# Two spills held back behind a weight load, four projection tiles issued in a row, and a split first pass over the output weights

## The reference

```python
x = x + attn(layernorm(x))      # a long convolution along the last axis (4096) with a kernel K
                                # computed from a 64-state model, plus D * u
x = x + ffn(layernorm(x))

def ffn(x):                     # K=64 experts of rank 16, top 16 of 64
    scores = x @ Wr.T
    top_vals, top_idx = top_k(scores, 16)
    G = scatter(softmax(top_vals))            # (rows, 64)
    h = einsum('nd,krd->nkr', x, A)           # (rows, 64, 16) = rows x 1024
    return 2.0 * einsum('nkr,kdr->nd', h * G[:, :, None], B)
```

## Time and profile before

| | |
|---|---|
| median of 3 runs | 1453.24 us (1449.32 to 1455.43) |
| profiled execution, own time | 1455.56 us |
| its span, slowest core (core 4) | 1453.9 us |
| the other cores' spans | 1441.7 to 1453.0 us |
| PE busy | 990.3 us (68%) |
| VectorE, ACT, POOL busy | 454.8, 193.8, 178.9 us |
| DMA | 186.60 MB, mean 128 GB/s |
| chain that ended last, by engine | PE 49%, DMA 13%, VectorE 11%, issue 9%, POOL 6% |

### The profile page before, as it was taken

One profiled execution on the slowest core, in us unless ns is written; L12 is line 12 of the kernel. 1 busy time (PEld: TensorE's weight loads), 2 busy tenths in 40 slices (PEclk: granted clock), 3 DMA queues, 4 the chain that ended last, 5 costly groups with the idle time before them and its releaser, 6 DMA issues.

```text
span 1453.9 us, 13339 instructions; the slowest of 8 cores (1441.7 to 1453.9 us)
## 1 busy us (share of the span) xinstructions
PE 990.3 (68%) x3837; PEld 395.3 (27%) x3837; DVE 454.8 (31%) x954; ACT 193.8 (13%) x402; POOL 178.9 (12%) x221
## 2 busy tenths in 40 slices
PE   1655347667676678355288768767876944999997
PEld 0133132112112222111133323322332411444443
DVE  2022126237337349302422132222212001334442
ACT  1300013342332433000100010010001000000000
POOL 6700000440440534000000000000000000000000
PEclk9855557879878889767688778977878976999999
DMA  6300006846638319998100030020006057679876
GB/s 119 137 0 0 7 1 231 290 145 214 231 134 269 101 37 225 214 168 215 74 1 0 0 116 1 0 84 33 0 1 108 9 138 214 224 282 302 287 268 251
DMA packets 28977, 186.60 MB, mean 128 GB/s; under 512 B 7976, under 2 KB 8745, under 8 KB 12906
## 3 DMA queue, kind: packets, MB, share of 16 engines
q1 hardware_dynamic: 9274, 84.52, 16.9%
q0 software_dynamic: 12720, 34.11, 13.7%
q10 hardware_dynamic: 6912, 67.11, 12.3%
HBM read 119.15 MB, written 83.89 MB: 140 GB/s over the span
## 4 chain that ended last, share of the span: by engine, by line
PE 49%; DMA 13%; DVE 11%; issue 9%; POOL 6%; another core or an unknown queue 5%; ACT 4%; DVEq 1%; ACTq 0%; POOLq 0%; SPq 0%
PE psA L978 16%; PE psA L1066 15%; DMA xsp_b<-U 7%; POOL sqs L272 4%; DMA Bt_hi<-bt_in 3%; PE ps L823 3%; DVE sqs L817 2%; PE psX L870 2%; DMA U<-u_in 2%; DVE cvt L727 2%; PE psA L711 1%; PE psS L688 1%; PE ps L277 1%; POOL wrt_b L369 1%
## 5 line engine op out<-in xcount | busy, mean ns | idle before, releaser
L978 PE MATMUL psA<-X,At_sb 128*128 128x512 bf16 x1024 | 252.8, 410 | 0.0
L1066 PE MATMUL psA<-htl_b,Bt_hi 128*128 128x512 bf16 x512 | 133.6, 383 | 42.2 <-DMA Bt_hi<-bt_in 42.2
L1073 DVE SCALAR_TENSOR_TENSOR XF<-psA,XF 128x512 f32<-128x512 f32 x128 | 88.5, 691 | 177.5 <-PE psA L1066 121.2
L978 PEld LDWEIGHTS psA<-X,At_sb 128*128 128x128 bf16 x1024 | 105.7, 105 | 138.9 <-issue 38.9
L272 POOL TENSOR_TENSOR sqs<-ubf 128x512 bf16<-128x512 bf16 x128 | 131.0, 1056 | 45.5 <-PE ps L277 31.4
L1066 PE MATMUL psA<-htl_a,Bt_lo 128*128 128x512 bf16 x512 | 132.5, 381 | 0.0
L264 PE MATMUL ps<-ubf,sumw 128*128 128x512 bf16 x128 | 61.0, 477 | 70.9 <-ACT ubf L259 70.8
L732 DVE TENSOR_TENSOR U<-U,cvt 128x512 f32<-128x512 f32 x128 | 89.9, 702 | 13.7 <-DVE cvt L727 0.5
L711 PE MATMUL psA<-ln1w,cm_T 128*128 128x512 bf16 x320 | 93.5, 391 | 0.0
L259 ACT CAST ubf<-U 128x512 bf16<-128x512 f32 x128 | 72.9, 615 | 154.8 <-PE ps L264 50.5
L727 DVE TENSOR_TENSOR cvt<-psA,Rb 128x512 f32<-128x512 f32 x128 | 87.6, 684 | 7.6 <-PE psA L717 7.6
(11 more groups left out here) (228 smaller groups left out, 694.6 us busy)
## 6 DMA issues: line engine op xcount, KB each, us to landing
U<-u_in SPq DMA_DIRECT2D x16, 2048.0 KB, 8.6
xsp_f<-U ACTq DMA_DIRECT2D x16, 2048.0 KB, 12.3
XF<-xsp_f SPq DMA_DIRECT2D x32, 1024.0 KB, 7.6
y_out<-XF ACTq DMA_DIRECT2D x32, 1024.0 KB, 7.4
xsp_b<-U POOLq DMA_DIRECT2D x16, 1024.0 KB, 12.9
X<-xsp_b SPq DMA_DIRECT2D x3, 4096.0 KB, 13.8
At_sb<-at_in POOLq DMA_DIRECT2D x32, 256.0 KB, 54.5
X<-xsp_b SPq DMA_DIRECT2D x2, 2048.0 KB, 11.7
```

The source lines that it names most:

```text
L978: P.op("tensor", lambda e, kr=kr, db=db, pb=pb, xb=xb: e.matmul(psA.ap()[:, pb * 512:(pb + 1) * 512], At_sb.ap()[:, db * 1024 + kr * 128:d ...
L1066: P.op("tensor", lambda e, d=d, kbo=kbo, kb=kb, pb=pb, s1=s1, bt=bt: e.matmul(psA.ap()[:, pb * 512:(pb + 1) * 512], bt.ap()[:, kbo * DM + ...
L1073: P.op("vector", lambda e, dd=dd, pb=pb, xf=xf: e.scalar_tensor_tensor(xf.ap()[:, dd * 512:(dd + 1) * 512], psA.ap()[:, pb * 512:(pb + 1) ...
```

## The change

Three edits.

1. In slice 3 of the convolution stage the spills of quarters 2 and 3, on ACT's and on POOL's queue, wait until all 16 transfers of `at2` have landed. SP's wait ahead of the load of slice 2 into X2[0] asks for 224 in place of 256 (slices 1 and 3 keep 256).
2. In slice 0 of the gated stage tiles 0 to 3 are issued as a block: their projection matmuls one after the other into the four banks of `psA` (with a wait for the gating before bank 3), then for each of the four the gate matmul into `psS`, ACT's copy and VectorE's product, then all eight preparation steps of slice 1. Tiles 4 to 7 go on as before, with two more waits for the products that free the banks.
3. In the first pass of the output stage tiles 0 to 3 use the four banks of `psA`: first the matmuls on `Bt_lo` for all four, then those on `Bt_hi`.

```diff
@@ convolution stage, after every second chunk @@
                 P.wait("scalar", "v_xe", vxe_b + 8 * (q + 1))
+                if s == 3 and q >= 2:
+                    P.wait("scalar", "at2", 16 * 16)
                 P.dma("scalar", lambda e, s=s, buf=buf, q=q: e.dma_start(
...
                 P.wait("gpsimd", "v_xe", vxe_b + 8 * (q + 1))
+                if s == 3 and q >= 2:
+                    P.wait("gpsimd", "at2", 16 * 16)
                 P.dma("gpsimd", lambda e, s=s, buf=buf, q=q: e.dma_start(
...
-        P.wait("sync", "spf", 256)
-        P.wait("sync", "spb", 256)
+        need2 = 224 if s % 2 == 0 else 256
+        P.wait("sync", "spf", need2)
+        P.wait("sync", "spb", need2)
@@ gated stage @@
-        for kr in range(8):
+        kr_start = 0
+        if s == 0:
+            kr_start = 4
+            for kr in range(4):
+                if kr == 3:
+                    P.wait("tensor", "gq", gq_done[0])
+                for db in range(NBLK):
+                    P.op("tensor", lambda e, kr=kr, db=db, xb=xb: e.matmul(
+                        psA.ap()[:, kr * 512:(kr + 1) * 512],
+                        At_sb.ap()[:, db * 1024 + kr * 128:db * 1024 + (kr + 1) * 128],
+                        blk_ap(xb, db), start=(db == 0), stop=False))
+                P.op("tensor", ...rank-1 correction..., inc="t_h")
+            for kr in range(4):
+                if kr >= 1:
+                    P.wait("tensor", "s_gp", kr)
+                P.op("tensor", ...gate matmul into psS..., inc="t_gr")
+                P.wait("scalar", "t_gr")
+                if kr >= 2:
+                    P.wait("scalar", "v_ht", kr - 1)
+                P.op("scalar", ...copy psS to grep..., inc="s_gp")
+                P.wait("vector", "t_h")
+                P.wait("vector", "s_gp")
+                P.op("vector", ...product into htl..., inc="v_ht")
+            for _ in range(8):
+                if nxt_steps:
+                    nxt_steps.pop(0)()
+
+        for kr in range(kr_start, 8):
...
+            if s == 0 and kr == 4:
+                P.wait("tensor", "v_ht", 3)
             P.wait("tensor", "gq", gq_done[s])
...
                 elif kr == 5:
+                    if s == 0:
+                        P.wait("tensor", "v_ht", 4)
                     sx_r2 = emit_chain2(s + 1, nb2)
@@ output stage @@
-        for dd in range(16):
+        if s2 == 0:
+            for dd in range(4):
+                if dd < 2:
+                    P.wait("tensor", "v_ht", htl_after[-1] - 1 + dd)
+                if dd == 0:
+                    P.wait("tensor", "btl", 16 * 4)
+                for kb in range(4):
+                    P.op("tensor", ...matmul on Bt_lo into bank dd, start=(kb == 0), stop=False...)
+            for dd in range(4):
+                for kb in range(4, 8):
+                    if dd == 0:
+                        P.wait("tensor", "bhi", 16 * (kb - 3))
+                    P.op("tensor", ...matmul on Bt_hi into bank dd, stop=(kb == 7)...,
+                        inc=("t_o" if kb == 7 else None))
+                P.wait("vector", "t_o")
+                P.wait("vector", "xfl", 16)
+                P.op("vector", ...residual add of bank dd..., inc="v_y")
+        for dd in range(4 if s2 == 0 else 0, 16):
```

More of the change, by code:

```diff
@@ L971, in build_nc @@
             nxt_steps, nb2 = emit_prep2(s + 1)
-        for kr in range(8):
+        kr_start = 0
[9 more added lines that the diff above has]
+                        blk_ap(xb, db), start=(db == 0), stop=False))
+                P.op("tensor", lambda e, kr=kr: e.matmul(
+                    psA.ap()[:, kr * 512:(kr + 1) * 512],
+                    A1row.ap()[0:1, kr * 128:(kr + 1) * 128],
+                    nm2.ap()[0:1, 0:512],
+                    start=False, stop=True), inc="t_h")
+            for kr in range(4):
+                if kr >= 1:
+                    P.wait("tensor", "s_gp", kr)
+                P.op("tensor", lambda e, kr=kr: e.matmul(
+                    psS.ap()[:, :], rghx.ap()[64:128, kr * 128:(kr + 1) * 128],
+                    ghx.ap()[64:128, 0:512], start=True, stop=True), inc="t_gr")
+                P.wait("scalar", "t_gr")
+                if kr >= 2:
+                    P.wait("scalar", "v_ht", kr - 1)
+                P.op("scalar", lambda e, kr=kr: e.copy(
+                    grep.ap()[:, (kr % 2) * 512:(kr % 2 + 1) * 512],
+                    psS.ap()[:, :]), inc="s_gp")
+                P.wait("vector", "t_h")
+                P.wait("vector", "s_gp")
+                P.op("vector", lambda e, kr=kr: e.tensor_mul(
+                    htl_ap(kr, 0, 512),
+                    psA.ap()[:, kr * 512:(kr + 1) * 512],
+                    grep.ap()[:, (kr % 2) * 512:(kr % 2 + 1) * 512]), inc="v_ht")
+            for _ in range(8):
+                if nxt_steps:
+                    nxt_steps.pop(0)()
+        for kr in range(kr_start, 8):
             pb = kr % 2
@@ L1050, in build_nc @@
         xf = XF[s2 % 2]
-        for dd in range(16):
+        if s2 == 0:
[5 more added lines that the diff above has]
+                for kb in range(4):
+                    P.op("tensor", lambda e, dd=dd, kb=kb: e.matmul(
+                        psA.ap()[:, dd * 512:(dd + 1) * 512],
+                        Bt_lo.ap()[:, kb * DM + dd * 128:kb * DM + (dd + 1) * 128],
+                        htl_ap(kb, 0, 512), start=(kb == 0), stop=False))
+            for dd in range(4):
+                for kb in range(4, 8):
+                    if dd == 0:
+                        P.wait("tensor", "bhi", 16 * (kb - 3))
+                    P.op("tensor", lambda e, dd=dd, kb=kb: e.matmul(
+                        psA.ap()[:, dd * 512:(dd + 1) * 512],
+                        Bt_hi.ap()[:, (kb - 4) * DM + dd * 128:(kb - 4) * DM + (dd + 1) * 128],
+                        htl_ap(kb, 0, 512), start=False, stop=(kb == 7)),
+                        inc=("t_o" if kb == 7 else None))
+                P.wait("vector", "t_o")
+                P.wait("vector", "xfl", 16)
+                P.op("vector", lambda e, dd=dd, xf=xf: e.scalar_tensor_tensor(
+                    xf.ap()[:, dd * 512:(dd + 1) * 512], psA.ap()[:, dd * 512:(dd + 1) * 512],
+                    2.0, xf.ap()[:, dd * 512:(dd + 1) * 512], ALU.mult, ALU.add), inc="v_y")
+        for dd in range(4 if s2 == 0 else 0, 16):
             d = 16 * g + dd
             pb = dd % 2
-            if s2 == 0 and dd < 2:
-                P.wait("tensor", "v_ht", htl_after[-1] - 1 + dd)
             if s2 * 16 + dd >= 2:
@@ L1060, in build_nc @@
                 kbo = kb % 4
[L1061 to L1065, removed]
                 P.op("tensor", lambda e, d=d, kbo=kbo, kb=kb, pb=pb, s1=s1, bt=bt: e.matmul(
```

## The result

The change is faster by 1.0%: a ratio of 0.9896 (95%: 0.9877 to 0.9914), which of 1453.6 us is 15.1 us (12.5 to 17.9). Ratios and intervals leave out slow executions, in which the cores of one half of the chip show a lower granted clock; of the ten after this was one, at 1532.4 us, and of the ten before none.

The account below looks back on a forecast made before the run. The load of X's second half bounds the gated stage's start, then PE with its helpers, then PE alone in the output. Gains 5 + 5.5 + 2.5 = 13.0 take 1455.56 to 1442.5 us (median 1440.2); range 1430 to 1450.

Parts of the forecast that it names:

- spills: Input of the gated stage: delayed spills let the load of X's second half land earlier; gain 5 us, bounds -4 and +10.
- tiles: Gated stage, slice 0: four tiles in a row, then gates and sums, 54.7 us for 60.2; gain 5.5, bounds 1.4 to 7.3.
- output: Output stage, first tiles: twelve matmuls run ahead of the last landing of B; gain 2.5 us, bounds 2.2 and 5.1.
- rival D: Gated stage, slice 0: low clock through all the sums; tiles gain 1.4 for 5.5, total 8.9, 1444.3 us; chance 0.12.
- E: Convolution's end: matrix A lands no faster, near 644, X's second half 11 us later; 1456 or 1463 us; chance 0.07.
- q 2 at once and q 3 when q 2 has landed: Tail of DMA behind matrix A: both delayed spills lie in it, adding 2 x 6.5 to 30.7 us, less 0 to 4.
- T: Convolution's end, slice 3: the time matrix A has landed, forecast about 628 us, 16 earlier; bounds 14 and 19 earlier.
- A: Whole kernel: the forecast itself holds, 1436 to 1444 us; chance 0.45.
- C: Tail of DMA: spills fill gaps, X's second half lands by 665; 10 or more, total 18, 1433 to 1436 us; chance 0.13.
- B: Tail of DMA: each spill costs 7 to 9 us; spills bring 0 to -4, total 4 to 8, 1445 to 1449; chance 0.2.
- I count five such pairs: Gated stage, slice 0: only five pairs of sum matmuls run at the low clock, 1.27 us apart against 1.03, adding 1.1.
- F: Gated stage, slice 0: four tiles run under the gating chain, PE's 15.67 us of waiting vanish; about 1425 us; chance 0.03.

Follow-up runs that it names:

- the early casts: The changed kernel with chunk 7's four casts issued on ACT ahead of its waiting spill: ratio 0.9899 to the kernel before, against the change's 0.9896.
- The two experiments on the clock: Changed kernel with each gate right behind its tile: ratio 0.9878 to the kernel before; changed kernel with slice 1's sums right behind tile 4's projection: 0.9859.

## Why the prediction was right, and where its sizes were off

The total was predicted at 13.0 and measured at 15.1. Each term in us against what it measured, on the slowest cores of the two profiled executions, as the mean of the cores, and by the edit alone:

| term | predicted | slowest cores | mean of the cores | edit alone |
|---|---|---|---|---|
| spills | 5 | 8.4 | 9.2 | 7.6 |
| tiles | 5.5 | 1.4 | 3.6 | 2.8 |
| output | 2.5 | 2.5 | 3.4 | 2.9 |
| sum | 13.0 | 12.3 | 16.2 | 13.3 |

The tiles' 1.4 is 60.2 - 58.1, less the 0.7 that tile 4 is longer (7.86 against 7.16). Its 3.6 is the time from the gating's last transpose to slice 1's scores, 69.5 before and 65.9 after. Two terms were off, in opposite directions, and the total is nearer than they are: that much of the agreement is luck. The clock did what rival D said, whose total was 8.9, and the spills gave back what this cost.

**When A lands: right.** "About 628" was worked out from the share of the bytes that A gets beside a spill, and 627.84 is in the row; in the mean of the cores A landed 16.1 us earlier, where 16 was forecast. That rules out E.

**The tail of DMA: mis-sized.** The step "q 2 at once and q 3 when q 2 has landed", each at 6.5, less up to 4 of unused share, gave 42 us from T to x2l. It was 38.7 (627.84 to 666.52), against 30.7 before: the two spills cost 8.0 together and not 11.3. That lies between A and C. Part of it is a reading: the share of 0.87 that gave "4 us of 30.7 unused" is that of 663 to 675 alone. From 644 to 663 the share was 0.77, so 5.9 us were unused, and with all of them the same sum gives 37.8. After, the shares of 1.00, 0.92 and 0.89 (626 to 640, to 655, to 667) leave 2.5 us unused. By these shares, and this is an estimate, the two spills filled 3.4 us of gaps and took 5.7 us of the engines each, where 6.5 was forecast. Delaying them until x2l showed the mechanism: what costs is what rides beside POOL's spills and the two loads of X. The prediction counted ACT's two spills and took POOL's quarter 2 as given, since nothing in the change moves it against the load. In the change it costs nothing new, but it is the dearest companion of that load: 4.5 us (11.64 against 7.16). B, with a tail of 45 us and more, didn't come: the tail kept 265 and 311 GB/s. The Trainium skill (DMA: Bandwidth & Descriptors, Queues, rings and completion order) has the engines take turns between queues packet by packet. The runs agree in so far as each transfer stretches the ones beside it (the load 7.16 us alone, 11.64 beside a spill); by how much for which size of packet no run here took apart.

**PE's late work is hidden: right.** The first half of the scores was ready for x2l with 8.27 us to spare, and the early casts brought nothing. That **POOL's wait is free** was right too, by the one execution without it.

**The four tiles: the block right, the sums not.** The four gates 1.2 apart are as predicted, and 750.73 to 756.98 is 6.25 against 2.56 + 3.7. The block of tiles took 31.8 against 30.1, its first tile partly under the low clock that follows the gating (0.92 over the block). The step that failed is "I count five such pairs". It took the five from the stretch behind one of before's short pauses, where only four pairs come at all before the next tile raises the clock again. That stretch couldn't show how long the low clock lasts without a tile behind it. All 16 pairs came at it: 20.1 us in place of 16.5 + 1.1. This is case D, whose price of 1.4 is what the profiled cores show. (That 1.4 doesn't take off the 0.25 of tile 4 before, as the forecast's own term does; with it the price is 1.7.) The rule that spoke for D (the Trainium skill, TensorE: Matmul & The Clock Gate, Why this matters for your kernels) says that idle gaps between bursts bring the low clock. The trace agrees, with 0.50 behind the 6.2 us in which PE was busy for 1.54, and D deserved more than 0.12. The two experiments on the clock then showed what the prediction had not asked. The length of the gate chain isn't the cause. With the wait ahead of the sums the low clock came on every core, at the latest behind the third pair, and without that wait on none.

**Order on PE: right.** The 15.67 us stayed, F didn't come, and moving three tiles ahead showed what it would have given.

**Output: right.** Tile 4 began 5.0 us behind the landing, with 13 matmuls in between, as predicted.

**What stays open.** Of the profiled executions' 20.0 us, 4.5 behind the last matmul and 1.7 in slices 1 to 3 have no cause shown. Why the mean of the cores gained 2.2 more than the slowest ones in the tiles wasn't followed. Nor was what brought the full clock back midway, on two cores when the gates stood inside the block, on three in the run without POOL's wait and on one with the spills behind x2l. The lowered count ahead of the load of slice 2 was never taken out by itself; it stands in SP's list behind slice 1's wait for 256.

## What to carry to other kernels

When a stage waits for one load, list everything that shares the DMA engines with the transfers behind it and order it by who waits for it: a spill that nobody needs yet belongs behind that load, not merely behind the one before it. Small matmuls that wait on another engine are better woven one by one into a dense stretch than gathered into a block of their own; woven, they cost their own time, and in a block they cost the pace of the other engine and, entered out of a wait, half the clock. If a block is unavoidable, place it so that PE comes into it from dense work (16.6 us for 20.1 here).

## What the runs showed of the hardware that was not expected

- Thirty-two sum matmuls, with PE waiting 0.25 to 0.46 us between the pairs, kept the full clock on all eight cores when they were entered straight out of a tile: 16.6 us at 1.00. Entered out of a wait of 2.2 us they had the low clock on all eight cores of the changed kernel: 20.1 us at 0.50. In all seven kernels with such a block behind a wait (56 cores) the low clock came at the latest behind the third pair, and on six of the cores the full clock came back midway.
- A 2 MB load took 7.16 us with nothing in flight on ACT's and POOL's queues and 11.64 beside one 1 MB spill of POOL's software queue, in which float32 is written as bf16. The 1 MB spill itself took 14.41 us beside one load and 19.54 beside a load and ACT's spills.
